# The last group by seven products, its scores in front of five of v's, probabilities on ScalarE and VectorE, and the values of group 1 in t's banks

## The reference, cut to what matters

```python
h = maximum(layernorm(x), 0)
output = h @ weight                       # called v in the kernel
alpha = (h @ wq) @ (h @ wk).T             # (h @ (wq @ wk.T)) @ h.T; h @ M is called t
alpha = maximum(alpha, 0) * (graph != 0)
alpha = softmax(alpha, axis=1)            # down each column
return x + alpha @ output
```

## Time and profile before

| what | value |
|---|---|
| device time, median of 3 runs | 421.05 us (421.01 to 421.43) |
| the profiled execution | 420.8 us, of which the span from first to last instruction is 419.0 us |
| granted clock of PE | 1.00 over the whole span |
| busy share of the span | PE 97%, POOL 71%, DVE 68%, ACT 60% |
| chain that ended last | PE 81%, POOL 9%, DMA 3%, DVE 3%, ACT 1% |

### The profile page before, as it was taken

How to read it: one execution, slowest core, us unless ns; L and a number is a source line. 1 busy time by engine, 2 the same in 40 slices (tenths; PEclk the granted TensorE clock), 3 DMA queues, 4 the chain that set the end, 5 groups by cost and what they waited for, 6 DMA issues and landing times.

```text
span 419.0 us, 9187 instructions
## 1 busy us (share of the span) xinstructions
PE 406.6 (97%) x3499; PEld 314.8 (75%) x3499; DVE 282.9 (68%) x504; ACT 253.3 (60%) x517; POOL 298.2 (71%) x315
## 2 busy tenths in 40 slices
PE   5999997999999999999999999999999999999996
PEld 4434543779889797979889797979889797978452
DVE  4786566475866768685876768676777677456353
ACT  4478774657485666667485666667586765523421
POOL 0379887979979797979879797979889796130320
PEclk9999999999999999999999999999999999999999
DMA  7965748996969797896978598996988599261022
GB/s 286 364 91 97 194 81 212 202 219 177 191 216 178 221 165 206 199 210 178 196 238 157 154 213 219 194 207 180 187 251 151 157 228 221 51 107 59 0 103 100
DMA packets 157368, 73.97 MB, mean 177 GB/s; under 512 B 131216, under 2 KB 139408, under 8 KB 157328
## 3 DMA queue, kind: packets, MB, share of 16 engines
q1 hardware_dynamic: 156752, 72.37, 75.5%
q10 hardware_dynamic: 576, 1.05, 0.7%
HBM read 24.12 MB, written 16.78 MB: 98 GB/s over the span
## 4 chain that ended last, share of the span: by engine, by line
PE 81%; POOL 9%; DMA 3%; DVE 3%; ACT 1%; SPq 1%; issue 1%; DVEq 0%; POOLq 0%; ACTq 0%
PE bank L1041 9%; PE bank L1027 9%; PE bank L1026 9%; PE bank L1042 9%; PE bank L1024 9%; PE bank L1039 9%; PE s_bank L1055 3%; PE s_bank L1053 3%; PE s_bank L1054 3%; POOL hn_lo L375 2%; PE bank L1060 2%; PE bank L1062 2%; PE bank L1061 2%; DMA x_sb<-in_x 2%; POOL hn_lo L401 2%; PE bank L1160 2%
## 5 line engine op out<-in xcount | busy, mean ns | idle before, releaser
L375 POOL TENSOR_TENSOR hn_lo<-h,hn_hi 128x512 f16<-128x512 f32 x64 | 73.4, 1159 | 41.0 <-ACT hn_hi L512 40.7
L502 ACT ACTIVATE h<-x_sb,shift,rstd 128x512 f32<-128x512 f32 x64 | 49.8, 803 | 51.4 <-POOL shift L370 51.4
L401 POOL TENSOR_TENSOR hn_lo<-s,hn_hi 128x512 f16<-128x512 f32 x52 | 58.6, 1159 | 0.0
L1024 PE MATMUL bank<-hT_hi,mt_hi 128*128 128x256 f16 x208 | 56.7, 273 | 0.0
L1027 PE MATMUL bank<-hT_hi,mt_lo 128*128 128x256 f16 x208 | 56.7, 273 | 0.0
L1041 PE MATMUL bank<-wt_lo,hT_hi 128*128 128x256 f16 x208 | 56.7, 273 | 0.0
L1042 PE MATMUL bank<-wt_hi,hT_lo 128*128 128x256 f16 x208 | 56.7, 273 | 0.0
L1026 PE MATMUL bank<-hT_lo,mt_hi 128*128 128x256 f16 x208 | 56.7, 273 | 0.0
L1039 PE MATMUL bank<-wt_hi,hT_hi 128*128 128x256 f16 x208 | 56.7, 273 | 0.0
L517 ACT ACTIVATE hn_hi<-s 128x512 f16<-128x512 f32 x52 | 32.5, 628 | 36.4 <-POOL s L390 23.9
L407 POOL TENSOR_TENSOR probs<-exps,row_inv 128x512 f32<-128x512 f32 x16 | 16.8, 1049 | 47.3 <-DVE row_inv L829 47.3
(11 more groups left out here) (142 smaller groups left out, 1153.4 us busy)
## 6 DMA issues: line engine op xcount, KB each, us to landing
x_sb<-in_x SPq DMA_DIRECT2D x16, 1024.0 KB, 5.5
out_h<-x_sb SPq DMA_DIRECT2D x64, 256.0 KB, 2.1
adj_sb<-in_adj SPq DMA_DIRECT2D x16, 256.0 KB, 5.4
w_sb<-in_L_gnn_weight SPq DMA_DIRECT2D x1, 1024.0 KB, 11.4
hn_lo<-in_L_gnn_wk ACTq DMA_DIRECT2D x2, 256.0 KB, 3.9
hn_lo<-in_L_gnn_wk SPq DMA_DIRECT2D x2, 256.0 KB, 3.7
hn_hi<-in_L_gnn_wq SPq DMA_DIRECT2D x2, 256.0 KB, 6.3
hn_hi<-in_L_gnn_wq ACTq DMA_DIRECT2D x2, 256.0 KB, 6.9
```

Of the source, the lines that this page charges most:

```text
L375: nc.gpsimd.tensor_tensor(hn_lo[:, s, b], h[:, b], hn_hi[:, s, b], ALU.subtract).then_inc(h_split, 1)
L401: nc.gpsimd.tensor_tensor(low, s32[:, f], high, ALU.subtract).then_inc(s_split, 1)
L502: nc.scalar.activation(h[:, b], x_sb[:, s, b], ACT.Relu, bias=shift[:, b:b + 1], scale=rstd[:, b:b + 1]).then_inc(h_made, 1)
L1024: nc.tensor.matmul(o, bh[:, k, cols], ah[:, :, k], start=first and c == 0 and k == 0, stop=False, skip_group_check=True)
```

## The change

1. The last group is made by seven products. POOL, ACT and SP therefore make, split and transpose its four sums in period 13 and 14 too. PE's order in it is: t's P1 and P5, v's P1, t's P2 and P6, v's P5, t's P7, P3, P4, the outs of group 14, the scores of group 15, then v's P6, P2, P7, P3, P4, and its outs, each of which waits for its own block of p_split and for two or four of the v_split.
2. normalise on POOL is removed. hi_of_p on ACT writes p_hi in four instructions of 128 columns, each with its row_inv as a scale pointer; lo_of_p on DVE writes p_lo in four instructions. They stand in every period: hi_of_p(g - 1) ahead of hi_of_t11(g), lo_of_p(g - 1) ahead of lo_of_t(g, 0). The buffer probs is gone.
3. v of group 1 is written to TA, TB, TE and VA, each as soon as t of group 1 is split out of it; the wait for the residual of group 0 moves behind v, in front of the scores of group 1. The order of ACT and DVE between group 0 and the first period is changed to match.
4. The first transposes: the high part of a block is transposed when hi_of_h has made it, without the wait for the low part, and blocks 2 and 3 go as one DMA for each part.

```diff
-            def transpose_first(b):
-
-                sp.wait_ge(h_split, b + 1)
-                sp.dma_start_transpose(hT_hi[:, 0, b], hn_hi[:, 0, b]).then_inc(hT0_landed[b], 16)
-                sp.dma_start_transpose(hT_lo[:, 0, b], hn_lo[:, 0, b]).then_inc(hT0_landed[b], 16)
+            def transpose_first(b, n, landed):
+
+                sp.wait_ge(h_hi_made, b + n)
+                sp.dma_start_transpose(hT_hi[:, 0, b:b + n].rearrange("p b k n -> p (b k) n"),
+                                       hn_hi[:, 0, b:b + n].rearrange("p b d -> p (b d)")).then_inc(landed, 16)
+                sp.wait_ge(h_split, b + n)
+                sp.dma_start_transpose(hT_lo[:, 0, b:b + n].rearrange("p b k n -> p (b k) n"),
+                                       hn_lo[:, 0, b:b + n].rearrange("p b d -> p (b d)")).then_inc(landed, 16)
...
-            for b in range(GB):
-                transpose_first(b)
+            transpose_first(0, 1, hT0_landed[0])
+            transpose_first(1, 1, hT0_landed[1])
+            transpose_first(2, 2, hT0_landed[2])
...
+            def hi_of_p(g):
+
+                act.wait_ge(inv_made, g + 1)
+                if later(g):
+                    act.wait_ge(out_filled, GB * g)
+                for b in range(GB):
+                    nc.scalar.activation(p_hi[:, b], exps[:, b], ACT.Copy, scale=row_inv[:, b:b + 1]).then_inc(p_hi_made, 1)
...
                 copy_p5_v(g)
+                hi_of_p(g - 1)
                 hi_of_t11(g)
...
             hi_of_h(2, 0, 3)
+            hi_of_p(0)
             hi_of_whole_t(1, 0)
...
             hi_of_whole_t(1, 2)
+            hi_of_whole_t(1, 3)
             hi_of_sum(2, 0, 2, S2)
             hi_of_sum(2, 0, 3, S4)
-            hi_of_whole_t(1, 3)
             hi_of_whole_v(1, 0)
-            for b in range(GB):
-                normalise_h(3, 3, b)
-                if b > 0:
-                    hi_of_h(3, 1, b - 1, turn(0, 1))
-            hi_of_h(3, 1, GB - 1)
+            normalise_h(3, 3, 0)
+            normalise_h(3, 3, 1)
             hi_of_whole_v(1, 1)
+            hi_of_h(3, 1, 0, turn(0, 1))
+            hi_of_h(3, 1, 1)
+            normalise_h(3, 3, 2)
             hi_of_whole_v(1, 2)
+            hi_of_h(3, 1, 2)
+            normalise_h(3, 3, 3)
+            hi_of_h(3, 1, 3)
             hi_of_sum(3, 1, 0, S1)
             hi_of_sum(3, 1, 1, S3)
             hi_of_whole_v(1, 3)
...
+            copy_p1_t(LAST)
             exponentials(LAST - 1)
-            for c in range(1, K):
-                hi_of_whole_t(LAST, c)
+            copy_p5_t(LAST)
+            copy_p1_v(LAST)
+            hi_of_p(LAST - 1)
+            hi_of_t11(LAST)
+            copy_p5_v(LAST)
+            hi_of_t22(LAST)
+            hi_of_t12(LAST)
+            hi_of_t21(LAST)
             exponentials(LAST)
-            for b in range(GB):
-                hi_of_whole_v(LAST, b)
+            hi_of_v11(LAST)
+            hi_of_p(LAST)
+            hi_of_v12(LAST)
+            hi_of_v22(LAST)
+            hi_of_v21(LAST)
...
+            def lo_of_p(g):
+
+                for b in range(GB):
+                    vec.wait_ge(p_hi_made, GB * g + b + 1)
+                    nc.vector.scalar_tensor_tensor(p_lo[:, b], exps[:, b], row_inv[:, b:b + 1], p_hi[:, b], ALU.mult,
+                                                   ALU.subtract).then_inc(p_split, 1)
...
                         mean_variance(g + 2, b)
+                lo_of_p(g - 1)
                 lo_of_t(g, 0, bank[TA][:], 0, 0)
                 sum_x_t(g)
                 sum_x_v(g)
...
             softmax_sum(LAST - 1)
+            lo_of_p(LAST - 1)
+            sum_x_t(LAST)
+            lo_of_t(LAST, 0, bank[TA][:], 0, 0)
+            sum_c22_t(LAST)
+            lo_of_t(LAST, 1, c22_t, 1, 1)
+            lo_of_t(LAST, 2, bank[TE][:], 0, 1)
+            for b in range(HG):
+                residual(LAST - 1, (LAST - 1) % UNROLL, b)
+            lo_of_t(LAST, 3, bank[TB][:], 1, 0)
+            for b in range(HG, GB):
                 residual(LAST - 1, (LAST - 1) % UNROLL, b)
             softmax_shift(LAST, LAST % 2, LAST // 2 + 1)
+            sum_x_v(LAST)
             softmax_sum(LAST)
+            sum_c22_v(LAST)
+            lo_of_v(LAST, 0, bank[VA][:], 0, 0)
+            lo_of_p(LAST)
+            lo_of_v(LAST, 1, bank[VE][:], 0, 1)
+            lo_of_v(LAST, 2, c22_v, 1, 1)
+            lo_of_v(LAST, 3, bank[VB][:], 1, 0)
...
             for b in range(GB):
-                pe.wait_ge(out_read, b + 1)
+                pe.wait_ge(t_split, K + b + 1)
                 whole_product_v(1, b)
+
+            pe.wait_ge(out_read, GB)
             scores(1, 1, quadrants=False)
 
-            pe.wait_ge(v_split, 2 * GB)
+            pe.wait_ge(v_split, GB + TE + 1)
```

More of the change, by code:

```diff
@@ L232, in graph_attention_kernel @@
         s_split = sem("s_split")
-        hT0_landed = [sem(f"hT0_landed{b}") for b in range(GB)]
+        hT0_landed = [sem(f"hT0_landed{b}") for b in range(3)]
         hT_landed = [sem(f"hT_landed{s}") for s in range(2)]
@@ L961, in _ @@
             softmax_shift(0, 0, 1)
-            for f in range(2, 4):
-                vec.wait_ge(wt_hi_made, f + 1)
-                nc.vector.scalar_tensor_tensor(wt_lo[:, f], wt32[:, f], w_scale[:], wt_hi[:, f], ALU.mult,
-                                               ALU.subtract).then_inc(wt_split, 1)
+            lo_of_wt(2)
             softmax_sum(0)
+            lo_of_p(0)
             lo_of_whole_t(1, 0)
+            lo_of_wt(3)
             for b in range(GB):
@@ L1215, in _ @@
                 period(g // UNROLL, g % UNROLL)
-            pe.wait_ge(hT_landed[LAST % 2], 2 * 16 * turn(LAST // UNROLL, LAST % UNROLL))
-            pe.wait_ge(v_split, GB * LAST)
-            for c in range(K):
-                whole_product_t(LAST, c)
-            pe.wait_ge(p_split, LAST)
-            pe.wait_ge(t_split, K * LAST + 1)
-            for b in range(GB):
-                product_out(LAST - 1, b)
-            pe.wait_ge(scores_read, LAST)
-            scores(LAST, LAST % 2, quadrants=False)
@@ L1227, in _ @@
-            for b in range(GB):
-                pe.wait_ge(out_read, GB * (LAST - 1) + b + 1)
-                whole_product_v(LAST, b)
-            pe.wait_ge(p_split, LAST + 1)
-            pe.wait_ge(scores_read, LAST + 1)
-            for b in range(GB):
-                pe.wait_ge(v_split, GB * LAST + b + 1)
+            s, turns, sum_turns = LAST % 2, turn(LAST // UNROLL, LAST % UNROLL), sum_turn(LAST // UNROLL, LAST % UNROLL)
+            pe.wait_ge(hT_landed[s], 2 * 16 * turns)
+            product_t(s, N_P1, bank[TA][:], True)
@@ new lines, in _ @@
+            pe.wait_ge(sT_landed[s], 2 * 16 * sum_turns)
+            product_t(s, N_P5, bank[TE][:], True)
+            pe.wait_ge(v_split, GB * LAST)
+            product_v(s, N_P1, bank[VA][:], True)
+            pe.wait_ge(t_copied, done(LAST, 1))
+            product_t(s, N_P2, bank[TA][:], False)
+            product_t(s, N_P6, bank[TB][:], False)
+            product_v(s, N_P5, bank[VE][:], True)
+            pe.wait_ge(t_summed, done(LAST, 1))
+            product_t(s, N_P7, bank[TB][:], False)
@@ new lines, in _ @@
+            product_t(s, N_P3, bank[TE][:], False)
+            pe.wait_ge(t_summed, done(LAST, 2))
+            product_t(s, N_P4, bank[TB][:], False)
+            outs(LAST - 1)
+            pe.wait_ge(out_read, GB * LAST - 2)
+            scores(LAST, s)
+            pe.wait_ge(v_copied, done(LAST, 1))
+            product_v(s, N_P6, bank[VB][:], False)
+            product_v(s, N_P2, bank[VA][:], False)
+            pe.wait_ge(v_summed, done(LAST, 1))
+            product_v(s, N_P7, bank[VB][:], False)
@@ L1234, in _ @@
+            product_v(s, N_P3, bank[VE][:], False)
+            pe.wait_ge(v_summed, done(LAST, 2))
+            product_v(s, N_P4, bank[VB][:], False)
+            pe.wait_ge(out_read, GB * LAST)
+            for b in range(GB):
+                pe.wait_ge(p_split, GB * LAST + b + 1)
+                pe.wait_ge(v_split, GB * LAST + (2 if b < HG else 4))
                 product_out(LAST, b)
```

112 lines of the change are left out of this document (46 added, 66 removed).

## The result

The changed kernel takes 416.5 us in the median (415.74 to 416.67, four runs) against 421.1 (421.01 to 421.43) on the same chip: a ratio of 0.9886, 95% interval 0.9869 to 0.9903. The forecast was 416.3. The profiled execution took 416.35 us, its span is 414.6 where it was 419.0.

A forecast was written before the change was run, and what follows sets the result against it. PE bounds the kernel, issuing without gaps from 90 us. Start 2.7 plus end 2.0 take 4.7 off the 419.0 span: 414.3; plus 1.8 for execution and 0.25 for the median, 416.3 us (own range 414.6 to 417.8, chance 0.65).

The forecast's parts named there:

- The walk: Last group: only outs(15) lose, 0.6 us; last residual at 28.1 instead of 30.14, kernel end 2.0 us earlier.
- the end gives nothing: Rival, last group: each handover missed by 0.7 us, so PE's 2.4 is gone; 418.3 us; chance 0.10.
- Middle periods: Periods after the start and before the last group: change 0, PE stays at 23.61 us.
- DVE may be 1.0 us later: Middle periods: DVE can be 1.0 us later than before at no cost, just what lo_of_p takes.
- The slower rival: Rival, each of 13 periods: DVE more than 1.0 us later stalls PE; 429 us; chance 0.06.
- the transposes: First transposes, before v(0, 2): of PE's 1.0 us wait all or nothing is saved, 0.9 taken.
- the wait at 65: Ahead of v(1): PE's wait for the residual of group 0 goes, 2.8 us saved.
- The first period's wait: Ahead of the first period: PE's wait goes, 0.6 us saved.
- Period 2: First period: lateness of ACT and DVE costs PE 1.9 us where 0.3 was lost before.
- the start is eaten up: Rival, start: group 3's chain moves up less than 3.2 us, start gives 0.5; 418.5 us; chance 0.14.
- part 3's walk: Start: POOL's group 3 chain, 9.7 us long, moves up 3.2, reaching ACT at 78.6 to 79.1.

The follow-up runs named there:

- p0_low_in_one: Changed kernel with group 0's low probabilities made by one DVE instruction of 512 columns, all with the first graph's scale (other numbers); 414.44 us, one run.
- pool_waits_for_p0: Changed kernel with POOL held until group 0's four low probabilities are made; 418.7 us, one run.
- p0_low_in_two: Changed kernel with group 0's low probabilities made by two DVE instructions of 512 columns instead of four of 128, same numbers; 415.49 us, ratio to before 0.9869.
- dve_plus1: Changed kernel with the low probabilities computed once more, into a tile nothing reads, ahead of the real ones; 417.34 us, one run.
- v1_in_v_banks: Changed kernel with group 1's whole v in v's own banks again, each product waiting for a residual of group 0; 422.38 us, ratio to before 1.0026.

## Why the prediction was right

**The last group.** The walk held almost to a tenth. sum_x_v was forecast at 18.9 after the group's start and came at 18.84 (402.73), sum_c22_v's end at 22.0 (405.87), hi_of_p(15) at 21.4 (405.33), outs(15) lost 0.76 where 0.6 was forecast, the end gained 2.08 where 2.0 was. The rival "the end gives nothing" asked for 0.7 missed at each handover; none was missed by more than 0.2.

**Probabilities, the prices.** hi_of_p was put at 1.3 and took 1.28. The estimate from the Trainium skill (VectorE: DVE Perf Modes, The TRN2 errata) was 1.2, and the trace agrees with it within 0.1:

```profile
405.33 1.28 ACT L609 ACTIVATE p_hi<-exps,row_inv 128x128 f16<-128x128 f32 x4
```

lo_of_p was put at 1.0 and took 1.10 in the periods. Beside POOL it was put at 1.5, and there the step failed: 4.33. I scaled a row of 512 columns (1158 ns against 676) down to 128, that is I took the excess for one by columns. It is one by instruction, as p0_low_in_one and pool_waits_for_p0 show. For PE this is worth some 0.9 to 1.6 us, by which B falls in p0_low_in_two and p0_low_in_one. It struck in group 0 alone, since in the periods POOL then has only its instructions of four columns.

**Middle periods.** Forecast 0, measured 0: each of periods 3 to 14 is 23.61. "DVE may be 1.0 us later" was right as far as dve_plus1 goes. sum_x_v now waits longer for PE than the 0.60 of the earlier trace rows:

```profile
252.91 0.70 DVE L806 TENSOR_TENSOR bank<-bank,spare 128x512 f32<-128x512 f32 x1 [1.46 <-PE bank L1081]
```

DVE has more work and yet more slack. From row_inv to sum_x_v it has 0.45 us more to do: lo_of_p, less 0.59, since the mask takes 0.43 now and took 1.02 (in later periods 1.19) beside POOL's normalise, which is gone. But row_inv comes 1.31 earlier, 5.95 us ahead of sum_x_v (246.96) where it was 4.64 (250.59): DVE masks the scores behind the last v_lo, which waits for the last v_hi; on ACT that one stands behind the third hi_of_sum, which waits for POOL and comes just as much earlier (241.09, before 244.72, where the same point of the period lies 2.32 earlier now). This earlier chain, which the prediction named and gave no price, is what pays for lo_of_p. The slower rival needed more than 1 us on top of lo_of_p.

**The start.** The sum was 0.9 + 2.8 + 0.6 + 0.3 - 1.9 = 2.7; measured 2.32. Term by term: the transposes gave 0.75 of 0.9; the wait at 65 gave its 2.8. v(1) starts on time, but 0.44 us is then lost within it, on lo_of_whole_t(1, 1), and 0.10 ahead of outs(0), for which lo_of_p(0) ends at 59.20; neither was in the walk, and p0_low_in_one, where lo_of_p(0) is short, has neither. The first period's wait fell by 0.25 and not by 0.6, for the same reason.

Period 2 lost 1.27 and not 1.9, in the order forecast: copy_p1_t(2) (0.63, its end put at 79.7 to 80.3 and seen at 81.49, with PE 1.1 later than thought), P2 of v, the fourth out. The place, the order and the cause, POOL's chain to hi_of_sum(3), were right, but its length was not. The prediction moved the whole chain up by 3.2 and kept its 9.7 us. Its head did move by 3.2 (68.97 against 72.16), its end only by 1.5 (80.37 against 81.85):

```profile
68.97 3.48 POOL L387 TENSOR_TENSOR hn_lo<-h,hn_hi 128x512 f16<-128x512 f32 x2 [2.63 <-ACT hn_hi L503]
```

These two took 2.38 before; now they run beside DVE's mt_lo. The next two, the sums S1 and S3, took 1.71 and 1.45, before 1.27 each. The rival "the start is eaten up" said that the chain would move up by less than 3.2, and that much of it came true; it gave ACT and layernorm_scales as reasons, and the trace shows the two engines in each other's way. PE came 1.1 late itself, so the loss was 0.6 smaller than forecast all the same. The errors of the start, about 1.0 too hopeful (0.15, 0.10, 0.44 and 0.35) and 0.6 too gloomy, partly cancel: that the start is right within 0.4 us, and the time within 0.2, is in part luck.

**What the sum could not say** is what a part is worth alone. The parts' worths when undone are 2.1 (last group), 5.8 (v of group 1, 1.7 of it the clock), 4.1 (probabilities) and 0.2 (transposes, not told from nothing): 12 us, where the whole change brings 4.6. Part 2 costs DVE its time early and frees POOL, and only part 3 makes DVE's lateness harmless. The forecast had put part 2's worth into part 3's walk, as the 3.2 us by which POOL's chain moves up.

## What to carry to other kernels

- Price a VectorE instruction that reads two SBUF tensors beside a busy GpSimd by the instruction, not by the column: where both ran, one instruction of 512 columns took 1.09 and 1.48 us, one of 128 took 1.24 to 1.42. Cut such work into few large pieces, or place it where GpSimd is idle.
- In a start-up where several engines take turns, a saved wait is worth only the distance to the next late chain: 0.75 us of better transposes left 0.2. Measure from a fixed event in the kernel, not from the span's start, from which the same product here began 24.59 to 25.75 us later; and look at two executions of the same code before a difference under 1 us is believed.
- A worth measured by undoing one part holds beside the other parts; parts that free and load the same engine must be judged together. Look at the granted clock behind a long wait, too: a part of what undoing part 3 costs is slower matmuls, not waiting.

## What the runs showed of the hardware

Beside POOL's tensor_tensor instructions of 1.2 to 1.3 us each, three of DVE's instructions of 128 columns with two SBUF inputs took 1.24 to 1.42 us each, alone 0.35 or less, and ended 0.15 us after POOL's; those of 512 columns ended 0.55 after it. The Trainium skill (SBUF — State Buffer, SBUF: two separate sides) states that VectorE with two SBUF inputs and GpSimd share a pair of ports by "an exclusive lock, not a bandwidth split", held for the whole instruction. The trace agrees: 4.33 us for four, 1.09 for one of the same columns, 1.22 for four with POOL held.

Behind 4.8 us in which PE was idle, its matmuls started 0.43 us apart for 3.6 us, at a granted clock of 0.54, and 0.22 apart again from 70.3 on (v1_in_v_banks); behind an idle time of 2.7 us they kept 0.22 and a clock of 1.00 (the kernel before).
